# Cross stage of a perceiver layer: two score groups back to back, Strassen products in three PSUM banks

## The chip, the cores and the metric

The kernel is one launch on one core of a Trainium2 chip. The metric is the device time in microseconds. Lower is better. TensorE is called PE here, VectorE DVE, ScalarE ACT, GpSimd POOL and SyncE SP, as in the profile.

## The reference

The program is one layer with three parts, each added to a residual stream `x` of 256 rows by 512 features: cross attention over a context of 25088 rows, self attention with a learned bias, and a mixture of 8 experts. The change touches the first part alone:

```
q = layernorm(x) @ Wq.T + bq          # 256 x 512, 8 heads of 64
k = ctx @ Wk.T + bk                   # 25088 x 512
v = ctx @ Wv.T + bv                   # 25088 x 512
attn = softmax(q k^T / sqrt(64))      # per head, over the 25088 rows
x = x + attn @ v
```

The functions are float32. The kernel carries each factor of a product as two float16 parts, high and low, and makes a product from three float16 matmuls (high by high, low by high, high by low).

## The kernel before, in words

**Tiling.** The context comes in 49 chunks of 512 rows. For each chunk PE makes K (512 features by 512 rows) and V (512 by 512). Each is a 2 by 2 block product made in the Winograd form of Strassen's scheme: seven products M1, M5, M6, M2, M7, M3, M4 in that order (`unit`, L1600), each of 12 matmuls of 256 columns, and block sums between them. A product adds onto what its PSUM bank holds, so the sums need few extra instructions: `seed` (ACT, L761) copies M1's bank into a second one, `copy_m5` (ACT, L774) takes M5 into the SBUF tile `m5_f`, `add_u4` (DVE, L1194) and `add_c22` (DVE, L1207) add it to others. The four result blocks C11, C22, C12, C21 are then split: `block_highs` (ACT, L782) writes the float16 high part and `block_lows` (DVE, L1179) the low part.

**Attention per chunk.** The 8 heads go in four groups of two (g = 0 to 3). For a group, `scores` (PE, L1660) makes the logits of two heads in two PSUM banks, each head on one half of the array's rows (64 by 128). `maxima` (DVE, L1159) finds the row maxima and updates the running one, `exps` (ACT, L807) takes the exponentials with their row sums (4 instructions), `p_highs` (ACT, L820) and `p_lows` (DVE, L1173) split the probabilities, SP transposes both parts by DMA into `pt_s` (`turn_p`, L463), and `weigh` (PE, L1680) multiplies them with V two groups later, into `ps_o`. `add_o` (DVE, L1213) adds a pair of groups to the accumulator after POOL has rescaled it.

**Context.** The sums and the splits of the chunk two steps ahead are made by POOL (`ctx_parts`, L583: four sums and seven low parts per chunk) with high parts from ACT (`ctx_highs`, L708). In its order POOL then does `rescale` (L610) and `step_max` (L628), whose `dmax` ACT needs for `alphas` (L799).

**Order.** A step c works on the attention of chunk c and the products of chunk c + 1, and has two halves: in h = 0 (the K half) the products of K stand between groups 0 and 1, in h = 1 (the V half) those of V between groups 2 and 3. The order on each engine is written out by hand in its own `step`, and every engine runs its list in order. What joins them are semaphores; the waits that matter here are

```
elif m == M4:                                   # PE, unit, L1617
    pe.wait_ge(c22_done, g - 1)
...
dve.wait_ge(p_high, NG * c + g + 1)             # DVE, p_lows, L1175
...
if n in (3, 5):                                 # POOL, ctx_lows, L578
    pool.wait_ge(t_high, 2 * k - 1 + n // 5)
...
act.wait_ge(dmax_done, n + 1)                   # ACT, alphas, L802
```

M4 waits for `add_c22` of its own half, since it adds onto a bank that `add_c22` reads. PSUM has eight banks: `ps_proj` has four (the Strassen products), `ps_s` two (scores) and `ps_o` two (outputs). Steps 0 to 47 have both scores and products; step 48, the last, is written out apart (`last_step`).

Of the kernel before, what the change touches and what calls it, by code (L numbers as in the profile page):

```python
# [156 lines left out]
def layer(nc, x, ctxt, wq, wk, wv, bv, cols, w_in_dram, wg, w1, w2, w3, out):  # L157
    with ExitStack() as ctx:
# [42 lines left out]
        m5_f = sb("m5_f", [P, 2, QUARTER], F32, cross)  # L201
        q_s = [sb(f"q_s{k}", [P, NG, T], F16, cross) for k in range(2)]
# [149 lines left out]
        def score_bank(c, g, head):  # L352

            return ps_proj[:, head, :] if isinstance(c, int) and c == LAST and g % 2 else ps_s[:, head, :]

# [46 lines left out]
        C11, C22, C12, C21 = (0, 0, 0), (3, 1, 1), (2, 0, 1), (1, 1, 0)  # L402
# [297 lines left out]
        def _(act):  # L700
# [1279 lines left out]
```

## Time and profile before

| | |
|---|---|
| median of 3 runs | 1519.84 us (1518.81 to 1520.62) |
| the profiled execution, its own time | 1517.86 us |
| its span | 1516.1 us |
| PE busy | 1452.8 us, 96% of the span |
| VectorE busy | 1298.2 us, 86% |
| ScalarE busy | 1254.2 us, 83% |
| GpSimd busy | 951.0 us, 63% |
| mean granted PE clock | 0.984 of full speed |
| one step of the cross stage (605.38 to 629.98) | 24.60 us |
| in it PE, VectorE, ScalarE, GpSimd busy | 24.60, 21.50, 21.86, 18.84 us |

The cross stage is about the first 1240 us. The last row but one is the distance between the same scores instruction of two steps, and the last row is the busy time of each engine in that stretch: PE has no idle time there, and the others have three to six microseconds each.

### The profile page before, as it was taken

Reading aid. Unit: us, or ns where it says so; the run is one execution under the profiler, and the core shown is the slowest. Engines: PE = TensorE matmul, PEld = TensorE weight load, DVE = VectorE, ACT = ScalarE, POOL = GpSimd, SP = SyncE. Lnnn points to the kernel's source line nnn. Section 1 sums busy time; section 2 is a strip of 40 time slices with the busy share of each in tenths; the row PEclk is TensorE's granted clock in tenths of the full one; section 3 lists DMA queues with packets and bytes.
Section 4 is the critical chain, followed back from the end, with each engine's and each line's share of the span. In section 5 each row is a group of like instructions: output and inputs, shape, how many; then the busy total and the mean of one; then the engine's idle time right before and its main releaser. Section 6 shows DMA issues by size and latency. Waiting matters only on the chain.

```text
span 1516.1 us, 47982 instructions
## 1 busy us (share of the span) xinstructions
PE 1452.8 (96%) x17942; PEld 1206.2 (80%) x17942; DVE 1298.2 (86%) x1768; ACT 1254.2 (83%) x3039; POOL 951.0 (63%) x980
## 2 busy tenths in 40 slices
PE   6999999999999999999999999999999887599999
PEld 5788888888888888888888888888888764377776
DVE  6788989888888888898888888888889887788995
ACT  4788888888888888888888888888988875666883
POOL 6586877778687878787777878787878522500000
PEclk9999999999999999999999999999999998699999
DMA  4357555565656565655556565656566578766991
GB/s 187 71 110 143 115 135 133 122 138 117 143 113 139 111 143 112 139 119 134 135 116 143 113 145 111 138 111 145 112 137 130 116 154 223 175 232 241 337 329 46
DMA packets 460175, 220.40 MB, mean 145 GB/s; under 512 B 433856, under 2 KB 440000, under 8 KB 453328
## 3 DMA queue, kind: packets, MB, share of 16 engines
q1 hardware_dynamic: 459680, 218.22, 59.6%
q10 hardware_dynamic: 432, 1.32, 0.3%
q8 instruction: 43, 0.70, 0.2%
q14 instruction: 20, 0.16, 0.0%
HBM read 111.96 MB, written 0.56 MB: 74 GB/s over the span
## 4 chain that ended last, share of the span: by engine, by line
PE 85%; DVE 6%; DMA 3%; ACT 2%; POOL 2%; issue 1%; SPq 0%; DVEq 0%; ACTq 0%; POOLq 0%
PE ps_proj L1626 55%; PE ps_s L1676 9%; PE ps_o L1694 8%; PE ps_proj L1895 6%; PE ps_o L1911 3%; DMA pt_s<-p_s 2%; DVE wsp L1375 2%; PE ps_proj L1655 1%; POOL ctx_s L580 1%; DVE cmax L1163 1%; DVE p_s L1176 1%; PE ps_proj L1911 1%; DMA ctx_f<-ctxt_dram 1%; ACT prob L815 0%; PE ps_o L1596 0%
## 5 line engine op out<-in xcount | busy, mean ns | idle before, releaser
L1626 PE MATMUL ps_proj<-ctx_s,wk_s 128*128 128x256 f16 x4032 | 480.6, 273 | 3.9 <-ACT ps_proj L769 3.6
L1626 PE MATMUL ps_proj<-wv_s,ctx_s 128*128 128x256 f16 x4032 | 480.6, 273 | 1.5 <-ACT ps_proj L771 1.5
L580 POOL TENSOR_TENSOR ctx_s<-t_f,ctx_s 128x512 f16<-128x512 f32 x192 | 265.0, 1390 | 279.9 <-ACT ctx_s L717 279.9
L1626 PEld LDWEIGHTS ps_proj<-ctx_s,wk_s 128*128 128x128 f16 x4032 | 379.9, 98 | 66.4 <-issue 24.3
L1626 PEld LDWEIGHTS ps_proj<-wv_s,ctx_s 128*128 128x128 f16 x4032 | 379.9, 98 | 63.4 <-issue 11.4
L815 ACT ACTIVATE prob<-ps_s,nmax 128x256 f32<-128x256 f32 x776 | 357.1, 476 | 8.3 <-DVE nmax L1170 8.1
L1163 DVE TENSOR_REDUCE cmax<-ps_s 128x4 f32<-128x1024 f32 x194 | 237.5, 1224 | 123.9 <-PE ps_s L1676 123.9
L1176 DVE SCALAR_TENSOR_TENSOR p_s<-prob,p_s 128x1024 f16<-128x1024 f32 x196 | 320.3, 1634 | 0.7 <-ACT p_s L826 0.7
L580 POOL TENSOR_TENSOR ctx_s<-ctx_f,ctx_s 128x512 f16<-128x512 f32 x144 | 215.7, 1498 | 10.3 <-ACT ctx_s L712 5.4
L826 ACT ACTIVATE p_s<-prob 128x1024 f16<-128x1024 f32 x196 | 206.6, 1054 | 6.7
L1694 PE MATMUL ps_o<-v_s,pt_s 128*128 128x64 f16 x4704 | 171.6, 194 | 15.2 <-DMA pt_s<-p_s 15.2
L1694 PEld LDWEIGHTS ps_o<-v_s,pt_s 128*128 128x128 f16 x4704 | 165.2, 99 | 23.0 <-DMA pt_s<-p_s 17.8
L1676 PE MATMUL ps_s<-k_s,q_s 64*128 64x256 f16 x2328 | 160.7, 271 | 2.7 <-ACT prob L815 2.6
L815 ACT ACTIVATION_READ_ACCUMULATOR prob<-ps_s,nmax 128x1 f32 x776 | 161.6, 208 | 0.0
L1676 PEld LDWEIGHTS ps_s<-k_s,q_s 64*128 64x128 f16 x2328 | 97.5, 94 | 52.9 <-issue 39.1
L1185 DVE TENSOR_TENSOR v_s<-ps_proj,v_s 128x512 f16<-128x512 f32 x192 | 127.5, 686 | 11.4 <-ACT v_s L791 7.9
L1375 DVE SCALAR_TENSOR_TENSOR wsp<-wst,wsp 128x1024 f16<-128x1024 f32 x95 | 116.9, 1240 | 9.7 <-ACT wsp L947 9.4
L791 ACT ACTIVATE v_s<-ps_proj 128x512 f16<-128x512 f32 x192 | 108.9, 600 | 16.4 <-PE ps_proj L1626 16.4
L566 POOL TENSOR_TENSOR t_f<-ctx_f,t_f 128x512 f32<-128x512 f32 x48 | 104.8, 2184 | 0.0
L622 POOL TENSOR_TENSOR o_acc<-o_acc,alpha 128x512 f32<-128x512 f32 x98 | 103.0, 1051 | 0.0
L717 ACT ACTIVATE ctx_s<-t_f 128x1024 f16<-128x1024 f32 x96 | 100.6, 1048 | 0.1
L947 ACT ACTIVATE wsp<-wst 128x1024 f16<-128x1024 f32 x96 | 99.3, 1046 | 0.0
(235 smaller groups left out, 1800.4 us busy)
## 6 DMA issues: line engine op xcount, KB each, us to landing
ctx_f<-ctxt_dram SPq DMA_DIRECT2D x48, 1024.0 KB, 5.4
wst<-w_dram SPq DMA_DIRECT2D x96, 512.0 KB, 5.5
pt_s<-p_s SPq DMA_TRANSPOSE x408, 3.1
tisa<-tisa_scores SPq DMA_DIRECT2D x12, 256.0 KB, 5.7
w_in_f<-w_in_dram SPq DMA_DIRECT2D x2, 1024.0 KB, 6.2
w_f<-wk_dram SPq DMA_DIRECT2D x2, 512.0 KB, 6.4
ctx_f<-ctxt_dram SPq DMA_DIRECT2D x2, 512.0 KB, 7.8
w_f<-wv_dram SPq DMA_DIRECT2D x1, 1024.0 KB, 11.3
```

Source lines behind the costliest of these rows:

```text
L566: pool.tensor_tensor(out=t2, in0=b22, in1=t1, op=ALU.subtract).then_inc(t_sum, 1)
L580: pool.tensor_tensor(out=low[:, n, :, :], in0=sources[n], in1=high[:, n, :, :], op=ALU.subtract).then_inc(ctx_low, 1)
L791: ins = act.activation(out_v(0, odd, i, j), ps, ACT.Copy)
L815: ins = act.activation(prob[:, g % 2, (2 * b + r) * HC:(2 * b + r + 1) * HC], score_bank(c, g, b)[:, r * HC:(r + 1) * HC], ACT.Exp, bias=n ...
L826: act.activation(p_s[:, g % 2, 0, :], prob[:, g % 2, :], ACT.Copy, scale=P_SCALE).then_inc(p_high, 1)
L1163: dve.tensor_reduce(cmax[:, g % 2, :], ps.rearrange("p b (r k) -> p (b r) k", r=2), AX, ALU.max).then_inc(cmax_done, 1)
L1176: dve.scalar_tensor_tensor(out=p_s[:, g % 2, 1, :], in0=prob[:, g % 2, :], scalar=P_SCALE, in1=p_s[:, g % 2, 0, :], op0=ALU.mult, op1=ALU. ...
L1185: ins = dve.tensor_tensor(out_v(1, odd, i, j), ps, out_v(0, odd, i, j), ALU.subtract)
L1375: dve.scalar_tensor_tensor(out=weights(1, j)[:, n, :], in0=wst[:, j % 4, n, :], scalar=FW_SCALE, in1=weights(0, j)[:, n, :], op0=ALU.mult, ...
L1626: ins = pe.matmul(ps_proj[:, bank(h, role), sub * QUARTER:(sub + 1) * QUARTER], lhsT, rhs, start=(fresh and sub == 0 and t == 0 and i == 0 ...
L1676: ins = pe.matmul(score_bank(c, g, head)[:, r * HC:(r + 1) * HC], q_s[a][rows, g, r * P:(r + 1) * P], k_s[odd][b][rows, g, r * HC:(r + 1) ...
L1694: ins = pe.matmul(ps_o[:, vg // 2, col:col + DK], pt_s[:, vg, a, 4 * head + tile, :], v_s[vodd][b][:, tile, u * DK:(u + 1) * DK], start=(i ...
```

## The change

- **Scores.** Groups 2h and 2h + 1 are scored back to back, the even one in `ps_s`, the odd one in `ps_o` (`score_banks`). PE's half step becomes M1, scores, scores, M5, M6, weigh, M2, weigh, M7, M3, M4.
- **Outputs.** `weigh` writes one bank, `ps_proj[3]`, for both pairs (`out_bank`), and waits for the `add_o` of the pair before.
- **Strassen.** The products use three banks. M5 goes to the bank of role 2 and waits for the C21 low part of the half before; C22 is summed into the SBUF tile `c22_f`.
- **ScalarE.** Per half: C21, alphas, seed, context high, copy of M5, both groups' exps, C11, p_highs of the even group, the high part of the context sums (`sum_highs`, split off `ctx_highs`), p_highs of the odd group, C22, C12. p_highs of the odd group stood in the next half before.
- **VectorE.** Per half: C21, add_o, both maxima, add_u4, p_lows of the even group, add_c22, C11, p_lows of the odd group, C22, C12.
- The last step follows the same banks; the bias scores and the dummy matmuls of `keep_busy` move to other banks.

```diff
+        c22_f = sb("c22_f", [P, 2, QUARTER], F32, cross)
...
-        def score_bank(c, g, head):
...
+        def score_banks(c, g):
+
+            if isinstance(c, int) and c == LAST and g >= 2:
+                return (ps_proj[:, 0:2, :], ps_s[:, :, :])[g - 2]
+            return (ps_s[:, :, :], ps_o[:, :, :])[g % 2]
+
+        def out_bank(c, half):
+
+            return ps_o[:, 0, :] if isinstance(c, int) and c == LAST and half else ps_proj[:, 3, :]
...
-        M1, M5, M6, M2, M7, M3, M4 = (0, 0, 0), (3, 3, 3), (4, 4, 1), (1, 1, 0), (5, 5, 1), (6, 2, 2), (2, 6, 1)
+        M1, M5, M6, M2, M7, M3, M4 = (0, 0, 0), (3, 3, 2), (4, 4, 1), (1, 1, 0), (5, 5, 1), (6, 2, 2), (2, 6, 1)
...
-                g, ps = 2 * k + h, half_bank(bank(h, role))
+                g, ps = 2 * k + h, c22_f[:, :, :] if which == C22 else half_bank(bank(h, role))
...
-                    if strassen:
-                        seed(c + 1, h)
-                    pc, pg = back(c, 2 * h, 1)
-                    if exists(pc, 0):
-                        p_highs(pc, pg)
                     if exists(c, -1) and h == 0:
                         alphas(c - 1, 1)
                     if exists(c, 0) and h == 1:
                         alphas(c, 0)
                     if strassen:
+                        seed(c + 1, h)
+                    if exists(c, 2):
+                        ctx_highs(c + 2, odd, h)
+                    if strassen:
                         copy_m5(c + 1, h)
                     if exists(c, 0):
                         exps(c, 2 * h, odd)
+                        exps(c, 2 * h + 1, odd)
+                    if strassen:
+                        block_highs(c + 1, h, C11, 1 - odd)
                     if exists(c, 0):
                         p_highs(c, 2 * h)
-                    if strassen:
-                        block_highs(c + 1, h, C11, 1 - odd)
                     if exists(c, 2):
-                        ctx_highs(c + 2, odd, h)
+                        sum_highs(c + 2, odd, h)
                     if exists(c, 0):
-                        exps(c, 2 * h + 1, odd)
+                        p_highs(c, 2 * h + 1)
...
-                dve.tensor_tensor(half_bank(bank(h, 3)), half_bank(bank(h, 1)), m5_f[:, :, :], ALU.add).then_inc(c22_done, 1)
+                dve.tensor_tensor(c22_f[:, :, :], half_bank(bank(h, 1)), m5_f[:, :, :], ALU.add).then_inc(c22_done, 1)
...
-                    if exists(c, 0):
-                        maxima(c, 2 * h, odd)
-                    pc, pg = back(c, 2 * h, 1)
-                    if exists(pc, 0):
-                        p_lows(pc, pg)
-                    if strassen:
-                        add_u4(c + 1, h)
                     if exists(c, -1):
                         add_o(c - 1, h)
                     if exists(c, 0):
+                        maxima(c, 2 * h, odd)
                         maxima(c, 2 * h + 1, odd)
+                    if strassen:
+                        add_u4(c + 1, h)
+                    if exists(c, 0):
+                        p_lows(c, 2 * h)
                     if strassen:
                         add_c22(c + 1, h)
                         block_lows(c + 1, h, C11, 1 - odd)
                     if exists(c, 0):
-                        p_lows(c, 2 * h)
+                        p_lows(c, 2 * h + 1)
...
                 elif m == M5:
-                    pe.wait_ge(block_low, 4 * g - 2 + (2 if isinstance(k, int) and g == 2 else 0))
+                    pe.wait_ge(block_low, 4 * g)
...
-                elif g >= 1 or after(c, -1):
+                elif g % 2 == 0 and (g or after(c, -1)):
                     pe.wait_ge(exp_done, NG * c + g)
...
-                if vg % 2 == 0 and after(vc, -1):
-                    pe.wait_ge(added, 2 * vc + vg // 2 - 1)
+                if isinstance(vc, int) and vc == LAST and vg == 2:
+                    pe.wait_ge(exp_done, NG * LAST + 2)
+                elif vg % 2 == 0 and (vg or after(vc, -1)):
+                    pe.wait_ge(added, 2 * vc + vg // 2)
...
+                    units(M1)
+                    if exists(c, 0):
+                        scores(c, 2 * h, odd)
+                        scores(c, 2 * h + 1, odd)
+                    units(M5, M6)
+                    weighted(0)
+                    units(M2)
+                    weighted(1)
+                    units(M7, M3, M4)
```

**VectorE, the K half inside the loop.** L1163 and L1169 are the maxima, L1170 and L1176 (of the change) the running maximum, L1211 and L1217 `add_c22`, L1188 and L1194 the C11 lows, L1176 (before) and L1182 `p_lows`. Buffer numbers are left out of the names here and in the profile: `m_f` is `m5_f`, `c_f` is `c22_f`. Before:

```order
L1161 REGISTER_ALU
L1163 TENSOR_REDUCE cmax<-ps_s 128x4 [waits s_done]
L1170 SCALAR_TENSOR_TENSOR nmax<-cmax,nmax 128x2x2 [waits cmax_done]
L1210 REGISTER_ALU
L1211 TENSOR_TENSOR ps_proj<-ps_proj,m_f 128x512 [waits unit_done]
L1183 ISA
L1188 SCALAR_TENSOR_TENSOR k_s<-ps_proj,bk_s,k_s 128x256 [waits block_high]
L1188 SCALAR_TENSOR_TENSOR k_s<-ps_proj,bk_s,k_s 128x256
L1176 SCALAR_TENSOR_TENSOR p_s<-prob,p_s 128x1024 [waits p_high]
L1183 REGISTER_ALU
L1191 TENSOR_TENSOR k_s<-ps_proj,k_s 128x2x256 [waits block_high]
L1183 REGISTER_ALU
```

The change:

```order
L1176 SCALAR_TENSOR_TENSOR nmax<-cmax,nmax 128x2x2 [waits cmax_done]
L1203 ISA
L1204 REGISTER_ALU [waits unit_done]
L1207 SCALAR_TENSOR_TENSOR ps_proj<-ps_proj,bk_d,m_f 128x256 [waits m5_done]
L1207 SCALAR_TENSOR_TENSOR ps_proj<-ps_proj,bk_d,m_f 128x256
L1182 SCALAR_TENSOR_TENSOR p_s<-prob,p_s 128x1024 [waits p_high]
L1216 REGISTER_ALU
L1217 TENSOR_TENSOR c_f<-ps_proj,m_f 128x512 [waits unit_done]
L1189 ISA
L1194 SCALAR_TENSOR_TENSOR k_s<-ps_proj,bk_s,k_s 128x256 [waits block_high]
L1194 SCALAR_TENSOR_TENSOR k_s<-ps_proj,bk_s,k_s 128x256
L1182 SCALAR_TENSOR_TENSOR p_s<-prob,p_s 128x1024 [waits p_high]
```

`add_c22` stood right behind the maxima of the odd group. It now stands behind `p_lows` of the even group, which waits for `p_high`.

**ScalarE, the K half inside the loop.** L815 and L822 are the exps, L826 and L833 `p_highs`, L794 and L801 the C11 highs, L712 the context highs, L717 and L724 the highs of the context sums. Before:

```order
L815 ACTIVATE prob,lsum<-ps_s,nmax 128x256 [waits scaled]
L815 ACTIVATE prob,lsum<-ps_s,nmax 128x256 x3
L826 ACTIVATE p_s<-prob 128x1024 [waits turned_p2,exp_done]
L789 REGISTER_ALU
L794 ACTIVATE k_s<-ps_proj,bk_s 128x256 [waits unit_done]
L794 ACTIVATE k_s<-ps_proj,bk_s 128x256
L711 ISA
L712 ACTIVATE ctx_s<-ctx_f 128x1024 [waits ctx_loaded0]
L716 ISA
L717 ACTIVATE ctx_s<-t_f 128x1024 [waits t_sum]
L809 REGISTER_ALU
L815 ACTIVATE prob,lsum<-ps_s,nmax 128x256 [waits nmax_done]
```

The change:

```order
L822 ACTIVATE prob,lsum<-ps_s,nmax 128x256 x3
L816 REGISTER_ALU
L822 ACTIVATE prob,lsum<-ps_o,nmax 128x256 [waits nmax_done]
L822 ACTIVATE prob,lsum<-ps_o,nmax 128x256 x3
L796 REGISTER_ALU
L801 ACTIVATE k_s<-ps_proj,bk_s 128x256 [waits unit_done]
L801 ACTIVATE k_s<-ps_proj,bk_s 128x256
L832 ISA [waits exp_done]
L833 ACTIVATE p_s<-prob 128x1024 [waits turned_p2]
L723 ISA
L724 ACTIVATE ctx_s<-t_f 128x1024 [waits t_sum]
L833 ACTIVATE p_s<-prob 128x1024 [waits turned_p3,exp_done]
```

The even group's `p_highs` stood right behind its own four exps; eight exps and the C11 highs now stand ahead of it. The highs of the context sums stand behind it.

**PE, the end of the K half, of the change.** L1700 is `weigh`, L1629 the products M2, M7, M3 and M4 (the last row):

```order
L1629 MATMUL ps_proj<-ctx_s,wk_s 128x256 [waits ctx_low]
L1629 MATMUL ps_proj<-ctx_s,wk_s 128x256 x11
L1700 MATMUL ps_proj<-v_s,pt_s 128x64 [waits turned_p3]
L1700 MATMUL ps_proj<-v_s,pt_s 128x64 x23
L1611 REGISTER_ALU
L1629 MATMUL ps_proj<-ctx_s,wk_s 128x256 [waits u4_done,ctx_low]
L1629 MATMUL ps_proj<-ctx_s,wk_s 128x256 x11
L1611 REGISTER_ALU
L1629 MATMUL ps_proj<-ctx_s,wk_s 128x256 [waits ctx_low]
L1629 MATMUL ps_proj<-ctx_s,wk_s 128x256 x11
L1611 REGISTER_ALU
L1629 MATMUL ps_proj<-ctx_s,wk_s 128x256 [waits c22_done,ctx_low]
```

The products M7, M3 and M4 are now consecutive; M4 waits for `c22_done`, as before.

## Rows read from the trace of the kernel before

**Rows 1.** Stretch; busy of PE, PEld, DVE, ACT, POOL; PEclk, DMA share, GB/s.

```profile
605.38:629.98 24.60, 24.60 (x313) 20.93 (x312) 21.50 (x29) 21.86 (x56) 18.84 (x20) 1.00 0.58 128
```

**Rows 2.** Chain of waits, half a step; columns: start, us, what, instructions.

```profile
647.86 0.76 PE ps_s L1676 x12
648.62 2.73 PE ps_proj L1626 x24
651.34 0.70 PE ps_o L1694 x24
652.04 2.62 PE ps_proj L1626 x24
```

**Rows 3.** Timeline, PE, last step: two score groups back to back, then another.

```profile
1238.05 0.83 PE L1676 MATMUL ps_s<-k_s,q_s 64*128 64x256 f16 x12
...
1238.71 0.82 PE L1676 MATMUL ps_proj<-k_s,q_s 64*128 64x256 f16 x12
...
1239.46 1.89 PE L1587 MATMUL ps_proj<-tisa_e,tsel 128*16 128x512 f32 x4
```

**Rows 4.** Timeline, K half, PE and ScalarE; columns: start, us, engine, line.

```profile
642.48 0.81 ACT L769 ACTIVATE ps_proj<-ps_proj,bk_s 128x256 f32<-128x256 f32 x2 [0.80 <-DVE v_s L1185]
...
643.05 2.79 PE L1626 MATMUL ps_proj<-ctx_s,wk_s 128*128 128x256 f16 x24
...
644.15 0.21 ACT L805 ACTIVATE alpha<-dmax 128x8 f32<-128x8 f32 x1
...
644.65 0.60 ACT L780 ACTIVATE m_f<-ps_proj 128x512 f32<-128x512 f32 x1 [0.29 <-PE ps_proj L1626]
```

**Rows 5.** Timeline, ScalarE, later in the same half.

```profile
648.11 0.82 ACT L794 ACTIVATE k_s<-ps_proj,bk_s 128x256 f16<-128x256 f32 x2
...
648.82 1.05 ACT L712 ACTIVATE ctx_s<-ctx_f 128x1024 f16<-128x1024 f32 x1
...
649.77 1.05 ACT L717 ACTIVATE ctx_s<-t_f 128x1024 f16<-128x1024 f32 x1
...
650.71 0.47 ACT L815 ACTIVATE prob<-ps_s,nmax 128x256 f32<-128x256 f32 x1
...
652.51 1.59 ACT L796 ACTIVATE k_s<-ps_proj 128x512 f16<-128x512 f32 x3
```

**Rows 6.** Timeline, same half: VectorE beside GpSimd.

```profile
643.76 1.27 POOL L563 TENSOR_TENSOR t_f<-ctx_f 128x512 f32<-128x512 f32 x1
...
644.51 0.54 DVE L1170 SCALAR_TENSOR_TENSOR nmax<-cmax,nmax 128x4 f32<-128x4 f32 x1
...
649.92 0.16 DVE L1170 SCALAR_TENSOR_TENSOR nmax<-cmax,nmax 128x4 f32<-128x4 f32 x1
...
650.07 0.70 DVE L1211 TENSOR_TENSOR ps_proj<-ps_proj,m_f 128x512 f32<-128x512 f32 x1
...
651.08 3.25 POOL L580 TENSOR_TENSOR ctx_s<-t_f,ctx_s 128x512 f16<-128x512 f32 x2
...
651.46 1.85 DVE L1176 SCALAR_TENSOR_TENSOR p_s<-prob,p_s 128x1024 f16<-128x1024 f32 x1
```

**Rows 7.** VectorE's p_lows, 500 to 1000 us: duration ns min/median/max.

```profile
L1176 DVE SCALAR_TENSOR_TENSOR p_s<-prob,p_s x81: 1209/1840/2374, 503.8 to 996.0; 128x1024 f16<-128x1024 f32 x81
```

**Rows 8.** Timeline, GpSimd: end of the K half, and the V half.

```profile
655.60 0.20 POOL L635 TENSOR_TENSOR dmax<-nmax 128x8 f32<-128x8 f32 x1
...
662.50 1.16 POOL L580 TENSOR_TENSOR ctx_s<-t_f,ctx_s 128x512 f16<-128x512 f32 x1 [5.58 <-ACT ctx_s L717]
...
663.61 2.19 POOL L580 TENSOR_TENSOR ctx_s<-ctx_f,ctx_s 128x512 f16<-128x512 f32 x1
...
668.20 0.20 POOL L635 TENSOR_TENSOR dmax<-nmax 128x8 f32<-128x8 f32 x1
```

**Rows 9.** Two stretches outside the steady part; PE busy, PEclk, DMA share, GB/s.

```profile
1190.00:1202.00 12.00, 10.41 (x135) 1.00 0.41 78
1298.00:1310.00 12.00, 4.44 (x136) 0.50 0.80 132
```

More of the change, by code:

```diff
@@ L399, in out_v @@
             return v_s[odd][kk][:, 2 * j:2 * j + 2, i * QUARTER:(i + 1) * QUARTER]
-        C11, C22, C12, C21 = (0, 0, 0), (3, 1, 1), (2, 0, 1), (1, 1, 0)
+        C11, C22, C12, C21 = (0, 0, 0), (None, 1, 1), (2, 0, 1), (1, 1, 0)
         def half_bank(n):
@@ L715, in ctx_highs, with sum_highs @@
                     act.activation(ctx_s[odd][0][:, 2, :, :], ctx_f[odd][:, 2:4, QUARTER:CH], ACT.Copy).then_inc(ctx_high, 1)
+            def sum_highs(k, odd, half):
                 act.wait_ge(t_sum, 4 * k - 1 + half)
@@ L1181, in block_lows @@
                 role, i, j = which
-                g, ps = 2 * k + h, half_bank(bank(h, role))
+                g, ps = 2 * k + h, c22_f[:, :, :] if which == C22 else half_bank(bank(h, role))
                 dve.wait_ge(block_high, 4 * g + 1 + (C11, C22, C12, C21).index(which))
@@ L1218, in add_o @@
                 acc = o_acc[:, half, :, :, :].rearrange("p u r d -> p (u r d)")
-                dve.tensor_tensor(acc, acc, ps_o[:, half, :], ALU.add).then_inc(added, 1)
+                dve.tensor_tensor(acc, acc, out_bank(c, half), ALU.add).then_inc(added, 1)
             def by_rows(t, half):
@@ L1295, in last_step @@
                 block_lows(LAST, 1, C21, LAST % 2)
+                add_o(LAST - 1, 0)
                 maxima(LAST, 0, LAST % 2)
-                p_lows(LAST - 1, 3)
                 maxima(LAST, 1, LAST % 2)
-                add_o(LAST - 1, 0)
                 tisa_scores()
                 p_lows(LAST, 0)
+                maxima(LAST, 2, LAST % 2)
                 add_o(LAST - 1, 1)
-                maxima(LAST, 2, LAST % 2)
                 p_lows(LAST, 1)
@@ L1712, in units, with weighted @@
                                 unit(c + 1, 1 - odd, h, m)
-                    for half, before, between, behind in ((0, (M1,), (M5, M6), (M2,)), (1, (), (M7, M3), (M4,))):
-                        g = 2 * h + half
-                        units(*before)
-                        if exists(c, 0):
-                            scores(c, g, odd)
-                        units(*between)
-                        vc, vg = back(c, g, PV_LAG)
-                        if exists(vc, 0):
-                            weigh(vc, vg, odd if g >= PV_LAG else 1 - odd)
-                        units(*behind)
+                    def weighted(half):
+                        vc, vg = back(c, 2 * h + half, PV_LAG)
+                        if exists(vc, 0):
+                            weigh(vc, vg, odd if 2 * h + half >= PV_LAG else 1 - odd)
+                    units(M1)
[7 more added lines that the diff above has]
+                    units(M7, M3, M4)
             def last_step():
@@ L1729, in last_step @@
                 scores(LAST, 1, odd)
+                scores(LAST, 2, odd)
                 tisa_scores()
                 weigh(LAST - 1, 2, 1 - odd)
-                scores(LAST, 2, odd)
                 weigh(LAST - 1, 3, 1 - odd)
@@ L1742, in keep_busy @@
                 for _ in range(count):
[L1743 removed]
+                    pe.matmul(ps_proj[:, 0, :], w_in_s[K][0][:, 0, 0:P], w_in_s[K][0][:, 1, :], start=True, stop=True)
             pe.wait_ge(w_in_low[K], 2)
```

32 lines of the change are left out of this document (15 added, 17 removed).

## The prediction

> **What bounds the kernel now.** I read the stretches first. In one step of the cross stage's steady part PE is busy in all of its 24.60 us, at the full granted clock, while VectorE is busy for 21.50, ScalarE for 21.86 and GpSimd for 18.84 [rows 1]. So a step lasts as long as its PE instructions. The question for the change is therefore double: how much PE time it removes, and whether PE still finds everything ready. The chain of waits gives PE's pieces [rows 2]: one score group 0.76 us, 24 product matmuls 2.73 us when a score group stands ahead of them and 2.62 us otherwise (1.31 a product), a weigh 0.70. The timeline gives the durations on the other engines and, more important, what starts when.
>
> **What PE saves.** A score group uses the array in halves of 64 rows and every other matmul here all 128, and the rows show a price at each change of form. In the last step two score groups already stand back to back: the first takes 0.66 us, the second 0.75 [rows 3]. So joining two groups saves 0.10 in the scores and 0.11 in the products behind them [rows 2], 0.21 per half, 0.4 per step. With nothing else, a step would take 24.2 us.
>
> **What the new order asks of the other engines.** The two order listings show the point. M4 must wait for `add_c22`. Before, VectorE did it right behind the odd group's maxima. Now `p_lows` of the even group is ahead of it, and that needs `p_highs` of the even group, which ScalarE reaches only after the copy of M5, eight exps and C11. All of this begins with the scores of the same half, and the next half's scores come behind M4. It is a closed loop, and PE is in it only for short pieces. Around it, starting at the end of `p_highs`:
> - `p_lows` 1.21 if GpSimd is out of its way [rows 7], and at that moment it is: it waits for `sum_highs`, the instruction behind `p_highs`;
> - `add_c22` 0.70 [rows 6];
> - M4 and M1, 1.31 each [rows 2], two score groups 1.41 [rows 3];
> - from M5's start to the start of its copy 1.60 [rows 4], the copy 0.50 to the next start (0.60, less the 0.10 by which ScalarE's instructions overlap, as 648.82 and 649.77 show [rows 5]);
> - eight exps 3.60, since four take 1.80 from first start to what follows [rows 5];
> - C11 0.72 in the K half, and 0.50 in the V half (one instruction, as the three at 652.51 take 1.59) [rows 5];
> - `p_highs` 1.05, of the same form as the context sums at 649.77 [rows 5].
>
> That is 13.2 us in a V half and 13.4 in a K half, or 26.6 a step, though PE has only 24.2 us of work. Seen from PE, M4 could start about 9.4 us after the scores (1.41 + 2.62 + 0.70 + 1.31 + 0.70 + 2.62) and `add_c22` ends at 1.41 + 1.60 + 0.50 + 3.60 + 0.72 + 1.05 + 1.21 + 0.70 = 10.8. **M4 waits 1.4 us in each half.** Next, M5 now waits for the C21 low of the half before. VectorE reaches it through `add_c22`, C11, `p_lows` of the odd group, C22, C12 and C21: five instructions of 0.6 to 0.7 like `add_c22` [rows 6] and one of 1.2 to 2.3 [rows 7], 4.5 to 5.6 us against PE's 4.7 (0.70 + 1.31 + 1.31 + 1.41). I add 0 to 0.7 a half for it and for handovers between engines, which the pieces above leave out, and take 13.5 for the half from K to V.
>
> **The second loop runs through GpSimd.** `sum_highs` moves behind eight exps and `p_highs`. In its order GpSimd can do `rescale` and `dmax` only after the low parts that wait for `sum_highs`, and the alphas, now ahead of the seed, of the context highs and of the copy of M5 on ScalarE, wait for `dmax`. In the V half GpSimd sat idle 5.58 us for the highs of the sums and then took from 662.50 to 668.40, 5.90 us, up to the end of `dmax` [rows 8]. From the V half to the K half the loop is 5.90, alphas 0.2 [rows 4], seed 0.71 (0.81 less the overlap) [rows 4], context highs 0.95 [rows 5], copy 0.50, exps 3.60, C11 0.72, `p_highs` 0.95, `sum_highs` 1.05: 14.6 us, more than the first loop's 13.2. From K to V it is 651.08 to 655.80, 4.72 [rows 6, 8], then 0.2, 0.5, 0.5, 0.5, 3.60, 0.50, 0.95, 1.05 (the seed and the context highs are half as large or one instruction there): 12.5, so there the first loop decides.
>
> VectorE and GpSimd also get into each other's way. The running maximum started at 644.51 and ended at 645.05, when GpSimd's sum from 643.76 ended (645.03); the next one, with GpSimd idle at its start, took 0.16 [rows 6]. `p_lows` took 1.21 at best and 1.84 in the middle [rows 7], and GpSimd's two low parts beside one took 3.25 [rows 6] where one alone takes 1.16 [rows 8]. The 5.90 already contains one such wait (2.19 instead of 1.16 [rows 8]). In the new K half the four context sums begin right after `dmax`, exactly when both running maxima come, on which the exps wait. Each may lose from nothing to one sum, 1.27 [rows 6]; together they delay the exps by 0 to 1.2. I take 0.7, and 15.3 us from V to K.
>
> The Trainium skill, page "SBUF — State Buffer", section "Who interferes with whom", says that a VectorE instruction with two SBUF inputs and a GpSimd instruction that reads SBUF take turns on a shared port, and that the later one waits for the whole of the other. The trace agrees, with the 0.54 and the 0.16. By that rule the added term may be all of 1.2; if the two only shared bandwidth, it would be nearly nothing.
>
> **Edits with no price of their own.** C22 in SBUF costs VectorE's sum the same 0.70 at most, and its low part gains a second SBUF input, which can cost up to one GpSimd instruction (in the range above). One output bank: `add_o` (about 0.7) stands at the start of VectorE's half, and weigh comes 4.0 us after the scores, so it is covered. The transposes of the even group have a whole half, those of the odd group some 6 us. ScalarE loses the idle 0.1 us between exps and `p_highs`; it isn't the bound. The last step has PE waiting on ScalarE already; one `p_lows` less and one group of exps earlier there are worth -2 to +2, taken as 0.
>
> **Sum.** 15.3 + 13.5 = 28.8 us a step against 24.60: +4.2, in the 46 steps that also prepare context (with step 0 counted apart, and step 47, which has no context work). 46 x 4.2 = 193, plus 2 x 2.4 for those two, by the first loop with handovers (27.0): +198 us. The profiled execution took 1517.86 (span 1516.1); it would take 1716. The median of the runs shown is 2 us above it, so **1718 us**. From both sides: with the first loop alone, and no handovers, 26.6 a step, 48 x 2.0 = +96, 1616; with every collision in both halves 15.8 + 14.1 = 29.9, 46 x 5.3 + 5 = +249, 1769.
>
> **Rivals.**
> - *Only the M4 loop counts.* GpSimd starts its lows early enough and nothing collides: 26.6 to 27.0 a step, 1616 to 1635. For it: GpSimd is busy only 18.84 of 24.60 us [rows 1]. Against it: that idle time was one wait for `sum_highs` [rows 8], and this instruction moves back. 14%.
> - *The change gives what PE saves.* M4 finds C22 ready and the step falls to 24.2: 48 x 0.4 = -19, 1501. This is the faster side. It decides if `add_c22` ends within 9.4 us of the scores, 1.4 less than my sum; the eight exps alone are 3.6 of it, with no slack to find. 4%.
> - *Something in between*, most of M4's wait absorbed: 1515 to 1610. 5%.
> - *PE's clock falls.* PE would be busy 24.2 of 28.8 us, 84%. At 87% the granted clock stayed 1.00, at 37% it was 0.50 [rows 9], that is 1.2 GHz instead of 2.4. The Trainium skill, "TensorE: Matmul & The Clock Gate", section "Part 1: The HAM clock gate", says that an idle PE is put back to the half clock. In rows: at a mean of 0.8 the 5.3 us of PE pieces in each half's loop grow by 1.3, 2.6 a step, +125, about 1840. The waits are short and spread, so 5%.
> - The forecast: 72%.
>
> **Numbers.** A difference of 0.2%, 3 us, is about what a measurement of this kernel can tell from none. Slower: 72 + 14 + 5 and most of the in-between, 94%; same 2%; faster 4%. The range goes from the first loop alone to all collisions, 1616 to 1769, rounded to 1620 and 1770; it leaves out the clock, the in-between and the faster case, 14%.
>
> **What would show it.** PE busy about 84% in the steady part, with PE idle ahead of one product per half, released by VectorE's `add_c22` (over 1 us each); VectorE idle some 3 us ahead of the even `p_lows`, released by ScalarE's `p_highs`; ScalarE idle ahead of the alphas, released by GpSimd's `dmax`; score groups back to back in 1.41 us; V to K scores further apart than K to V. I am wrong on the first loop if VectorE doesn't wait for `p_high`, on the second if alphas never wait, and wrong altogether if PE stays at 100% busy.

## The result and the profile after

The changed kernel takes **1762.78 us** (median of 4 runs, 1762.46 to 1772.35) against 1519.32 for the kernel before in the same session: ratio 1.1618, 95% interval 1.1578 to 1.1659. It is slower, as forecast. The forecast was 1718; the time lies inside the range of 1620 to 1770, near its upper end. The profiled execution took 1762.66 us, +244.8 on the one of before.

Stretches of the changed kernel, columns as in [rows 1]: a K half and a V half of one step, then those of a later step.

```profile
612.84:628.35 15.51, 12.30 (x157) 10.56 (x157) 11.96 (x16) 11.48 (x29) 12.55 (x14) 1.00 0.43 72
628.35:641.80 13.45, 12.39 (x157) 10.46 (x156) 10.08 (x14) 10.57 (x27) 6.32 (x7) 1.00 0.65 153
701.23:718.41 17.18, 13.97 (x157) 11.34 (x157) 13.60 (x19) 11.50 (x29) 14.21 (x17) 0.90 0.42 88
718.41:731.66 13.25, 12.26 (x157) 10.54 (x156) 8.50 (x11) 10.58 (x27) 4.65 (x4) 1.00 0.61 120
```

So there are two kinds of step: 28.96 us, and, in 19 of the 48, about 30.4. PE does the same work in both (157 matmuls a half). In the first kind it is busy for 12.3 us of 15.5 and for 12.4 of 13.4, 85% of the step, where 84% was forecast.

The waits of the changed kernel from 100 to 1400 us; columns: who waits, for whom, us in total, times, longest.

```profile
POOL ctx_s L584 <- ACT ctx_s L724: 467.8, 88, 8.6
DVE p_s L1182 <- ACT p_s L833: 296.9, 88, 3.7
ACT alpha L812 <- POOL dmax L639: 233.1, 87, 3.4
...
PE ps_proj L1629 <- DVE c_f L1217: 123.9, 86, 2.0
PE ps_proj L1629 <- DVE v_s L1191: 53.7, 43, 1.3
```

All three waits of the forecast are there in nearly every one of the about 90 halves: VectorE's `p_lows` for ScalarE, ScalarE's alphas for GpSimd, and M4 (PE for `c_f`) for VectorE. The last row is a fourth wait, of M5 for the C21 low part of the half before, in the K halves. The timeline shows how they hang together, in the K half that begins at 701.23 and the V half behind it.

```profile
701.23 0.83 PE L1680 MATMUL ps_s<-k_s,q_s 64*128 64x256 f16 x12
...
701.89 0.82 PE L1680 MATMUL ps_o<-k_s,q_s 64*128 64x256 f16 x12
...
703.96 2.78 PE L1629 MATMUL ps_proj<-ctx_s,wk_s 128*128 128x256 f16 x24 [1.25 <-DVE v_s L1191]
...
704.03 0.21 ACT L812 ACTIVATE alpha<-dmax 128x8 f32<-128x8 f32 x1 [3.41 <-POOL dmax L639]
...
705.91 0.60 ACT L787 ACTIVATE m_f<-ps_proj 128x512 f32<-128x512 f32 x1
...
706.60 0.47 ACT L822 ACTIVATE prob<-ps_s,nmax 128x256 f32<-128x256 f32 x1
...
711.87 1.10 ACT L724 ACTIVATE ctx_s<-t_f 128x1024 f16<-128x1024 f32 x1
...
712.06 1.22 DVE L1182 SCALAR_TENSOR_TENSOR p_s<-prob,p_s 128x1024 f16<-128x1024 f32 x1 [3.29 <-ACT p_s L833]
...
713.05 2.36 POOL L584 TENSOR_TENSOR ctx_s<-t_f,ctx_s 128x512 f16<-128x512 f32 x2 [2.89 <-ACT ctx_s L724]
...
714.03 2.43 PE L1629 MATMUL ps_proj<-ctx_s,wk_s 128*128 128x256 f16 x12 [1.96 <-DVE c_f L1217]
...
716.25 2.22 PE L1629 MATMUL ps_proj<-wv_s,ctx_s 128*128 128x256 f16 x12
...
718.41 0.83 PE L1680 MATMUL ps_s<-k_s,q_s 64*128 64x256 f16 x12
...
719.83 2.79 PE L1629 MATMUL ps_proj<-wv_s,ctx_s 128*128 128x256 f16 x24
...
726.86 1.11 ACT L724 ACTIVATE ctx_s<-t_f 128x1024 f16<-128x1024 f32 x1
...
728.94 1.48 PE L1629 MATMUL ps_proj<-wv_s,ctx_s 128*128 128x256 f16 x12 [0.99 <-DVE c_f L1217]
```

The two score groups take 1.42 us where M5 follows without a wait (718.41 to 719.83), 1.41 in [rows 3]. The alphas come 2.80 us behind the scores, the copy of M5 (705.91) 1.67 later than the 3.01 behind the scores that PE alone would allow, and M4 is late by 1.96. M4 and M1 then take 2.22 and 2.16 us from start to start: PE's granted clock, 0.90 over this half, is down here (0.61 from 714.03 to 718.41, 1.00 from 705 to 714). In the other kind of step the same two take 1.31 and 1.40:

```profile
625.64 1.47 PE L1629 MATMUL ps_proj<-ctx_s,wk_s 128*128 128x256 f16 x12 [1.96 <-DVE c_f L1217]
...
626.95 1.47 PE L1629 MATMUL ps_proj<-wv_s,ctx_s 128*128 128x256 f16 x12
```

### The profile page after: what moved, and what is told of

Its sections match the earlier page's. It is cut to its first block, busy times and chain, and to the rows that moved or that the text cites. A ratio compares the mean times of both kernels' runs of the same rounds, so it can differ in the third digit from the quotient of the medians.

```text
span 1760.9 us, 47836 instructions
## 1 busy us (share of the span) xinstructions
PE 1492.4 (85%) x17942; PEld 1234.1 (70%) x17942; DVE 1323.8 (75%) x1768; ACT 1262.3 (72%) x3039; POOL 953.9 (54%) x980
## 4 chain that ended last, share of the span: by engine, by line
issue 45%; POOL 34%; PE 12%; DVE 4%; ACT 2%; DMA 1%; POOLq 1%; SPq 1%; DVEq 0%; ACTq 0%
POOL ctx_s L584 19%; PE ps_proj L1905 5%; POOL l_acc L624 5%; POOL t_f L570 3%; POOL t_f L567 3%; PE ps_o L1921 2%; DVE wsp L1378 1%; PE ps_proj L1658 1%; POOL l_acc L629 1%; DMA pt_s<-p_s 1%; POOL dmax L639 1%; ACT prob L822 1%; PE ps_proj L1921 1%; DMA ctx_f<-ctxt_dram 1%; POOL t_f L572 0%
## 5 line engine op out<-in xcount | busy, mean ns | idle before, releaser
L1629 PE MATMUL ps_proj<-ctx_s,wk_s 128*128 128x256 f16 x4032 | 495.3, 278 | 156.2 <-DVE c_f L1217 93.9
L1182 DVE SCALAR_TENSOR_TENSOR p_s<-prob,p_s 128x1024 f16<-128x1024 f32 x196 | 313.8, 1601 | 328.9 <-ACT p_s L833 328.9
L1629 PEld LDWEIGHTS ps_proj<-ctx_s,wk_s 128*128 128x128 f16 x4032 | 387.4, 99 | 228.3 <-issue 180.6
L1629 PE MATMUL ps_proj<-wv_s,ctx_s 128*128 128x256 f16 x4032 | 502.4, 280 | 48.2 <-DVE c_f L1217 39.3
L1629 PEld LDWEIGHTS ps_proj<-wv_s,ctx_s 128*128 128x128 f16 x4032 | 392.2, 101 | 125.8 <-DVE c_f L1217 51.5
L833 ACT ACTIVATE p_s<-prob 128x1024 f16<-128x1024 f32 x196 | 216.2, 1105 | 0.3 <-DMA pt_s<-p_s 0.3
L822 ACT ACTIVATE prob<-ps_s,nmax 128x256 f32<-128x256 f32 x392 | 180.0, 475 | 9.6 <-DVE nmax L1176 4.8
L1700 PE MATMUL ps_proj<-v_s,pt_s 128*128 128x64 f16 x4656 | 168.9, 194 | 17.3 <-DMA pt_s<-p_s 17.1
L1700 PEld LDWEIGHTS ps_proj<-v_s,pt_s 128*128 128x128 f16 x4656 | 161.7, 98 | 27.1 <-DMA pt_s<-p_s 21.7
L822 ACT ACTIVATE prob<-ps_o,nmax 128x256 f32<-128x256 f32 x388 | 179.9, 499 | 0.0
L584 POOL TENSOR_TENSOR ctx_s<-ctx_f,ctx_s 128x512 f16<-128x512 f32 x144 | 167.1, 1160 | 3.9 <-ACT ctx_s L716 3.9
L1169 DVE TENSOR_REDUCE cmax<-ps_s 128x4 f32<-128x1024 f32 x98 | 119.2, 1216 | 8.1 <-PE ps_s L1680 8.1
L1169 DVE TENSOR_REDUCE cmax<-ps_o 128x4 f32<-128x1024 f32 x97 | 118.1, 1217 | 0.0
L724 ACT ACTIVATE ctx_s<-t_f 128x1024 f16<-128x1024 f32 x96 | 106.0, 1104 | 0.0
L624 POOL TENSOR_TENSOR l_acc<-l_acc,alpha 128x8 f32<-128x8 f32 x98 | 87.4, 892 | 28.1 <-ACT alpha L812 28.1
L1191 DVE TENSOR_TENSOR v_s<-ps_proj,v_s 128x512 f16<-128x512 f32 x144 | 94.0, 677 | 0.0
```

Of the source, the lines that this page charges most:

```text
L584: pool.tensor_tensor(out=low[:, n, :, :], in0=sources[n], in1=high[:, n, :, :], op=ALU.subtract).then_inc(ctx_low, 1)
L624: pool.tensor_tensor(out=l_acc[:, cols], in0=l_acc[:, cols], in1=alpha[:, cols], op=ALU.mult).then_inc(l_step, 1)
L724: act.activation(ctx_s[odd][0][:, 3 + 2 * half:5 + 2 * half, :, :], t_f[:, 2 * half:2 * half + 2, :, :], ACT.Copy).then_inc(t_high, 1)
L833: act.activation(p_s[:, g % 2, 0, :], prob[:, g % 2, :], ACT.Copy, scale=P_SCALE).then_inc(p_high, 1)
L1169: dve.tensor_reduce(cmax[:, g % 2, :], score_banks(c, g).rearrange("p b (r k) -> p (b r) k", r=2), AX, ALU.max).then_inc(cmax_done, 1)
L1182: dve.scalar_tensor_tensor(out=p_s[:, g % 2, 1, :], in0=prob[:, g % 2, :], scalar=P_SCALE, in1=p_s[:, g % 2, 0, :], op0=ALU.mult, op1=ALU. ...
```

## Experiments

Every one is an edit of the changed kernel. Times of e1 to e8 and e10 to e12 are of one run; the kernel before took 1517.7 beside e1 to e4, 1519.1 beside e5 to e8, and 1517.3 (median of 17) beside e9 to e12. The four runs of the change lie 10 us apart, so a difference of a few us between single runs says nothing.

PE's clock has a part in most of these differences. Its mean over the span was 0.962 in the change, 0.938 in e1, 0.981 in e2, 0.937 in e3, 0.979 in e4, 0.958 in e5, 0.961 in e6, 0.980 in e7, 0.983 in e10, 0.982 in e11 and 0.962 in e12.

**e1: `add_c22` ahead of the even low part.**

```diff
-                    if exists(c, 0):
-                        p_lows(c, 2 * h)
                     if strassen:
                         add_c22(c + 1, h)
                         block_lows(c + 1, h, C11, 1 - odd)
+                    if exists(c, 0):
+                        p_lows(c, 2 * h)
```

> The change, but VectorE does add_c22 and the C11 low part ahead of p_lows of the even group. In the changed kernel M4 waited 1.96 us (K half) and 0.99 us (V half) for add_c22. Theory of two loops (the prediction's): M4's wait goes, but from V to K the loop through GpSimd (sum_highs, low parts, rescale, dmax, alphas) still sets the pace, and the later p_lows of the even group collide with GpSimd; a step stays between 28 and 29.4 us, the time between 1700 and 1760. Rival (M4's wait is the whole cost): the step falls by both waits, about 3 us, to 26 or less, the time below 1640.

Measured: **1814.5 us**, slower than the change by 52. Every theory missed upward. M4's wait is gone; M5's took its place (PE and VectorE from 600 to 634 us):

```profile
604.13 2.78 PE L1629 MATMUL ps_proj<-ctx_s,wk_s 128*128 128x256 f16 x24 [2.49 <-DVE v_s L1191]
...
618.49 4.27 PE L1629 MATMUL ps_proj<-wv_s,ctx_s 128*128 128x256 f16 x24 [2.21 <-DVE k_s L1197]
...
628.20 3.68 DVE L1182 SCALAR_TENSOR_TENSOR p_s<-prob,p_s 128x1024 f16<-128x1024 f32 x2
...
631.81 1.64 DVE L1191 TENSOR_TENSOR v_s<-c_f,v_s 128x512 f16<-128x512 f32 x1
```

The C22, C12 and C21 lows stand behind both `p_lows`, which now come late and together, beside GpSimd. M5 waits for C21, since with three banks it goes where C21 was. So VectorE's queue can close a third loop. It isn't alone here: the alphas still wait for `dmax`, up to 5.0 us.

Most of the 52 us seems to be the clock, though. In the V half shown M5 and M6 take 4.27 us, where 2.78 is usual (604.13). Its step is 14.63 and 16.03 us, and all steady steps of e1 last 30.6 to 30.7. Without the 1.5 us of the clock that would be about 29.2, an estimate from these rows, against 28.96 in the change.

**e2: GpSimd does `rescale` and `dmax` ahead of the lows that wait for the sums.** Only lows 0 and 1 stay ahead; the other five follow `step_max`.

> The change, but GpSimd does rescale and dmax ahead of the low parts that wait for sum_highs. Theory of two loops: ScalarE's wait for dmax ahead of the alphas (3.41 us in the K half, 1.34 in the V half) goes, but the M4 loop through VectorE's p_lows stays at 13.2 to 13.5 a half and the clock episodes with it; 26.6 to 29 us a step, 1625 to 1740. Rival (M4's wait is the whole cost and GpSimd only follows): nothing changes, 1763 within 5.

Measured: **1766.2 us**, no gain, although the alphas wait for `dmax` no more. From 300 to 1100 us (the line numbers are 6 higher here) the next instruction, the seed, waits instead, for VectorE's C12 low:

```profile
ACT ps_proj L782 <- DVE v_s L1197: 68.6, 27, 2.5
ACT ps_proj L784 <- DVE k_s L1203: 66.5, 27, 2.5
```

The halves are 15.26 and 14.41 us, 29.67 a step against 28.96. The wait for GpSimd had hidden one for VectorE of nearly the same length. The time is the same all the same, because the clock no longer falls: it is 1.00 from 200 to 1100 us, although M4 still waits up to 1.7 us and M5 up to 1.3.

**e3: both edits.**

> Both edits. Theory of two loops: each alone gives little and both together clearly more than the sum of their gains, 25 to 27.7 us a step, 1540 to 1670; what is left is ScalarE's and VectorE's own order and their collisions with GpSimd. Rival (one cause): the same as the better of the two edits alone.

Measured: **1816.5 us**. The seed waits up to 4.1 us, M5 up to 3.0, both for VectorE's lows; the mean clock is 0.937. M4 and the alphas wait no more. Halves in which the clock doesn't fall last 14.6 (K) and 14.4 us (V), 29.0 together. With two loops opened, the third alone is as slow as all, in this order of VectorE, which also puts the even low part back; e11 has the third loop by itself.

**e4: dummy matmuls in M4's wait.** They keep PE busy until `add_c22` is nearly done (M4 still waits up to 0.5 us); their results are not used.

```diff
-                    units(M7, M3, M4)
+                    units(M7, M3)
+                    if exists(c, 0) and exists(c, 1):
+                        pe.wait_ge(exp_done, NG * c + 2 * h + 2)
+                        for _ in range(14 if h == 0 else 7):
+                            pe.matmul(ps_s[:, 0, 0:QUARTER], wk_s[0][:, 0, 0, 0:P], wk_s[0][:, 1, 0, :], start=True, stop=True)
+                    units(M4)
```

> The change, with 14 dummy matmuls of 256 columns ahead of M4 in a K half and 7 in a V half, into a score bank that has been read, so that PE isn't idle while M4 waits. Their results are used by nobody. In the changed kernel K halves last 15.52 or, in runs of several steps, 17.18 us, and in the long ones M4 and the next M1 take 2.2 us instead of 1.3 and 1.4. Theory: the long ones are PE's clock falling to half after M4's wait; with the wait filled all K halves last about 15.5, a step 28.97, the time about 1730. Rival: the two lengths come from collisions of VectorE and GpSimd, or the dummies cost as much as they save; then 1755 to 1790.

Measured: **1737.4 us**, 25.3 less than the profiled execution of the change. In the steady part the halves are 15.54 and 13.46, 29.0 a step; the 30.4 us steps are gone. From 600 to 800 us the change had the clock at 0.97, e4 has 1.00:

```profile
600.00:800.00 200.00, 185.43 (x2305) 159.15 (x2304) 151.35 (x193) 151.72 (x390) 130.21 (x132) 1.00 0.51 109
```

This is the price of the clock by itself: the loops are as long as before, only PE's idle time is filled.

**e5: VectorE's odd low part behind C22 and C12** (ScalarE's order unchanged).

> The change, but VectorE does p_lows of the odd group behind the C22 and C12 low parts instead of ahead of them. The first two kernels left one thing in common: M5 of the next half waits for the C21 low part, which is behind both p_lows of its half. Theory of two loops (M4 and GpSimd; M5's wait a small term): little, 1735 to 1765. New theory (the binding loop is VectorE's queue as a whole: exps, p_highs, both p_lows, C22, C12, C21, M5, its copy, exps): C21 is not freed by this, since it still stands behind the odd p_lows at the start of the next half; so also little, 1730 to 1800. This run tells the place of C22 and C12 from that of C21.

Measured: **1777.7 us**. M5 waits 0.7 us at most now, the halves are 15.52 with 13.86 or 17.17 with 13.26. The alphas still wait up to 3.4 us and M4 up to 2.1: the other two loops are whole.

**e6: ScalarE rounds the even group between the two groups' exps.**

> The change, but ScalarE does p_highs of the even group between the two groups' exps, as the kernel before did; everything else as changed (scores back to back, three banks). p_lows of the even group, and behind it add_c22, can start 2.5 us earlier (1.80 + 0.72). M4 loop theory: M4's waits go entirely and a step loses the 3 us of them, to 26 or 27 us, about 1640. GpSimd or VectorE theory: sum_highs and the odd p_lows stay where they are, so the step stays at 28 to 29.5 and only the clock episodes may go: 1700 to 1745.

Measured: **1740.9 us**, 22 less. M4 no longer waits; M5 waits up to 2.2 for the C21 low and the alphas up to 4.0 for `dmax`.

**e7: the odd group put off.** Its exps come behind the even rounding, its rounding and low part in the next half as before the change, and the sum rounding stands ahead of the copy of M5. Besides, `add_c22` and C11 stand ahead of the even low part on VectorE, and the odd group's maxima behind `add_u4`.

> Same scores, banks and PE order as the change; ScalarE and VectorE reordered: p_highs and p_lows of the odd group go to the next half, right behind C21; sum_highs goes ahead of the copy of M5; exps of the odd group go behind p_highs of the even one; C11 and add_c22 go ahead of p_lows of the even group. Theory of VectorE's queue and GpSimd together: both loops are cut, PE is again busy nearly all the time, a step 24.2 to 25.5 us, the time 1500 to 1565. Rival (three banks and M5's wait for C21 are what costs): a step stays above 27, 1640 or more.

Measured: **1614.3 us**: halves of about 12.5 (K) and 13.8 us (V), clock 1.00 from 300 to 1100 us. The alphas wait no more. PE waits for the transposes of the odd group, which now come too late (up to 2.1 us for `pt_s`, 46.2 us in all from 300 to 1100 us).

**e8: three moves together.** The sum rounding goes first in the half, right behind the C21 high part; the even rounding goes between the groups' exps; the odd rounding and the odd low part go last in the half, behind C12. The context highs and the seed go ahead of the alphas with the sum rounding.

```
ScalarE: C21, sum_highs, ctx_highs, seed, alphas, copy of M5, exps even, p_highs even,
         exps odd, C11, C22, C12, p_highs odd
VectorE: C21, add_o, maxima, maxima, add_u4, p_lows even, add_c22, C11, C22, C12, p_lows odd
```

> Same scores, banks and PE order; sum_highs right behind C21 on ScalarE, exps of the odd group behind p_highs of the even one, p_highs and p_lows of the odd group last in their own half, add_c22 still behind the even p_lows. GpSimd theory: with sum_highs at the start its loop is cut, 24.5 to 26.5 us a step, 1515 to 1610. M5 theory (odd p_lows ahead of C21 keeps M5 waiting): above 27 a step, 1640 or more.

Measured: **1525.1 us** against 1519.1 before. The steady halves are 12.09 (V) and 12.22 or 12.42 (K), 24.42 us a step against the 24.60 of before. It lost the gain outside: in step 0 ScalarE waited 7.1 us for GpSimd's first sums, and in a late step 3.0 and 3.3 us for the bias table's preparation behind the odd low part.

**e9: e8 with those two places mended.**

```diff
+                    first = isinstance(c, int) and c == 0 and h == 0
+                    if exists(c, 2) and not first:
                         sum_highs(c + 2, odd, h)
...
+                    if exists(c, 2) and first:
+                        sum_highs(c + 2, odd, h)
                     if strassen:
                         block_highs(c + 1, h, C22, 1 - odd)
...
+                    if isinstance(c, int) and c == LOOP_END + 1:
+                        tisa_args(h)
                     if exists(c, 0):
                         p_lows(c, 2 * h)
```

In step 0 the sum rounding stands where it stood. In the late step VectorE prepares the bias table (`tisa_args`) ahead of the even low part, and ScalarE's exponential of it stands ahead of C11.

> The order of e8 (sum rounding first in a half, even split between the two exponentials, odd split last), with two places outside the steady stretch mended: in the first half of step 0 the sum rounding stands where it stood, since there ScalarE waited 7.1 us for GpSimd's sum (first half 22.5 us against 13.6 before), and the time-interval exponential of the one late step no longer stands behind the odd split (ScalarE waited 3.0 us there, PE 2.7). The steady halves of e8 were 12.09 and 12.22 to 12.43, 24.4 us a step against 24.60 before. If the steady gain of 0.18 us x 42 steps = 8 us was only covered by those two places (some 9 and 2 to 3 us), this gives 1511 to 1517, faster than before by 0.2 to 0.5%. Rival: the longer distance from the odd split to its transposes costs at both ends of the loop whatever is mended, 1519 to 1525.

Measured, in 12 runs beside 17 of the kernel before (1517.29): **1511.55 us** (1510.16 to 1515.04), ratio **0.9962, interval 0.995 to 0.9974**. It is faster than the kernel before, by 0.4%. Two steps of it:

```profile
605.21:654.21 49.00, 48.49 (x627) 42.52 (x626) 44.38 (x57) 43.45 (x113) 34.46 (x38) 1.00 0.59 127
```

24.50 us a step, of which PE works 24.24: the 24.2 that the prediction worked out as PE's part alone, against 24.60 [rows 1]. In 200 to 1100 us the one wait of PE that remains is

```profile
PE ps_proj L1637 <- DVE v_s L1196: 8.2, 19, 0.4
```

The next three each take one of the three moves back.

**e10: sum rounding late again.** The seed and the context highs go behind the alphas again too, as in the change; so this is two things at once, both on the second loop.

> e9 with one of its three moves taken back: the sum rounding stands behind both exponentials and the even split again. If the loop over GpSimd (sum rounding, GpSimd's lows, difference of maxima, alphas, seed, context rounding, exponentials) bounds by itself, alphas waits for the difference of maxima for 2 to 4 us in each half, the step is 26.5 to 28 and the time 1600 to 1690. If VectorE's queue (the odd split ahead of the C12 and C21 lows) was what really bound, no such wait stays and the time is within 10 us of e9.

Measured: **1724.1 us**, more than the 1690 expected; halves 15.13 and 13.9 to 14.1. In 200 to 1100 us:

```profile
ACT alpha L812 <- POOL dmax L639: 212.9, 62, 4.0
```

ScalarE waits for nothing else in this stretch, and the clock is 1.00. So from one sum rounding over GpSimd and the alphas to the next the loop is closed, 29.1 us a step.

**e11: odd group's rounding and low part ahead of C22 and C12 again.**

> e9 with another move taken back: the odd split of a half stands ahead of the C22 and C12 splits again on both engines, as in the change. If VectorE's queue bounds by itself, the seed waits for the C12 low, or the M5 product for the C21 low, 0.5 to 2 us a half, the step is 25.5 to 28 and the time 1560 to 1680. If the other two moves were what mattered, within 10 us of e9.

Measured: **1581.9 us**, halves of 12.83 to 13.29, 26.0 to 26.1 us a step; M5 waits up to 0.6 us for C21, M4 up to 0.8 for `c_f`.

**e12: even rounding behind both groups' exps again.**

> e9 with the third move taken back: ScalarE rounds the even group only behind the exponentials of both, as in the change. If the loop of the M4 product (even rounding, even low, C22 sum, M4, the rest of PE's half up to the scores, M5, its copy, eight exponentials, C11, rounding: 13.2 us by the sum of the prediction) bounds by itself, both halves are about 13.2, the step 26.4 and the time 1595 to 1615, with M4 waiting about 1 us for VectorE's sum in each half. If it had only been carried along by the other two, within 10 us of e9.

Measured: **1722.9 us**, 108 above the upper bound expected. The halves are 14.32 and 13.77, and 15.6 to 16.0 where the clock falls. One V half:

```profile
613.44 0.83 PE L1688 MATMUL ps_s<-k_s,q_s 64*128 64x256 f16 x12
...
616.38 0.60 ACT L787 ACTIVATE m_f<-ps_proj 128x512 f32<-128x512 f32 x1 [2.06 <-PE ps_proj L1637]
...
616.87 0.47 ACT L822 ACTIVATE prob<-ps_s,nmax 128x256 f32<-128x256 f32 x1
...
620.47 0.65 ACT L798 ACTIVATE v_s<-ps_proj 128x512 f16<-128x512 f32 x1
...
620.95 1.11 ACT L833 ACTIVATE p_s<-prob 128x1024 f16<-128x1024 f32 x1
...
622.10 2.21 DVE L1187 SCALAR_TENSOR_TENSOR p_s<-prob,p_s 128x1024 f16<-128x1024 f32 x1 [3.71 <-ACT p_s L833]
...
624.23 0.68 DVE L1222 TENSOR_TENSOR c_f<-ps_proj,m_f 128x512 f32<-128x512 f32 x1
...
624.97 1.48 PE L1637 MATMUL ps_proj<-wv_s,ctx_s 128*128 128x256 f16 x12 [1.98 <-DVE c_f L1222]
...
626.28 1.47 PE L1637 MATMUL ps_proj<-ctx_s,wk_s 128*128 128x256 f16 x12
...
627.69 0.83 PE L1688 MATMUL ps_s<-k_s,q_s 64*128 64x256 f16 x12
```

This is the first loop of the prediction, alone and closed: 2.94 + 0.49 + 3.60 + 0.48 + 1.15 + 2.13 + 0.74 + 1.31 + 1.41 = 14.25 us. The sum was 13.2; the one term that differs is `p_lows`, 2.21 instead of 1.21, since with the earlier sum rounding GpSimd is at work beside it (a sum of 1.27 us starts at 621.96). In the change GpSimd was waiting then. This V half is one of the longer ones, behind a fall of the clock. The usual ones of 13.77 us have a shorter collision:

```profile
652.30 1.64 DVE L1187 SCALAR_TENSOR_TENSOR p_s<-prob,p_s 128x1024 f16<-128x1024 f32 x1 [3.70 <-ACT p_s L833]
```

In the K half `p_lows` takes 1.22, and instead the exps wait 0.6 us for a running maximum of 1.0 to 1.1 us beside GpSimd's low parts. 28.1 us a step and the falls of the clock together make the miss.

## Why the prediction was right, point by point

- **PE's saving** was 0.4 us a step in the forecast. It is real: PE's busy time is 24.24 us a step in e9, and a half in which PE waits for nothing lasts 12.09 us there against 12.30 before, the 0.21 of the forecast.
- **First loop, M4 behind the even rounding.** The V half from 718.41 lasts 13.25 us; the sum was 13.2. M4's wait was put at 1.4 in each half and is 0.99 there, 1.96 in the K half. e12 shows that this loop bounds by itself.
- **Second loop, sum rounding, GpSimd, alphas.** From one sum rounding to the next it takes 14.99 us from K to V (711.87 to 726.86), and the rest of that 30.4 us step, 15.4, from V to K, where 15.3 was forecast. In the steps without a clock fall K to V is 13.52, with 13.5 forecast:

```profile
623.47 1.11 ACT L724 ACTIVATE ctx_s<-t_f 128x1024 f16<-128x1024 f32 x1
...
636.99 1.11 ACT L724 ACTIVATE ctx_s<-t_f 128x1024 f16<-128x1024 f32 x1
```

  e10 shows that it too bounds alone. In the prediction's signs I had its scores the wrong way round: the wait comes behind the K scores, so K to V scores are the far ones (15.5), not V to K.
- **Within it** the exps start 0.2 us after the copy of M5 allows, not the 0.7 of the collision term, while GpSimd's part grew, from the 5.90 read in [rows 8] to 6.40 (728.04 to 734.44, its low parts in the V half up to the end of `dmax`). In it `rescale`'s first instruction, 128 by 8 elements, takes a median of 0.92 us in the changed kernel and 0.20 before (300 to 1100 us):

```profile
L624 POOL TENSOR_TENSOR l_acc<-l_acc,alpha x54: 646/916/1191, 301.1 to 1090.3; 128x8 f32<-128x8 f32 x54
```

```profile
L620 POOL TENSOR_TENSOR l_acc<-l_acc,alpha x65: 198/202/206, 309.8 to 1097.2; 128x8 f32<-128x8 f32 x65
```

  The first line is of the changed kernel, the second of the kernel before. Behind the V half's sums it now meets VectorE's C22 low part, which reads `c22_f` in SBUF, and behind the K half's the odd low part:

```profile
700.98 1.64 DVE L1191 TENSOR_TENSOR v_s<-c_f,v_s 128x512 f16<-128x512 f32 x1
...
702.03 0.65 POOL L624 TENSOR_TENSOR l_acc<-l_acc,alpha 128x8 f32<-128x8 f32 x1
...
714.58 1.91 DVE L1182 SCALAR_TENSOR_TENSOR p_s<-prob,p_s 128x1024 f16<-128x1024 f32 x1
...
715.37 1.18 POOL L624 TENSOR_TENSOR l_acc<-l_acc,alpha 128x8 f32<-128x8 f32 x1
```

  Both times it ends just behind VectorE's instruction (702.68 and 702.62, 716.55 and 716.49). The two deviations, -0.5 and +0.5, nearly cancel, which is luck. By the Trainium skill, "SBUF — State Buffer", section "Who interferes with whom", one of the two engines waits for the other's whole instruction; these rows agree, and show that it can be GpSimd that waits.
- **Step and sum.** From the scores of step 0 to those of the last step it is 1433.3 us, against 1191.0 before: +242.3. A step is 28.96 measured, 28.8 forecast: 46 x 4.36 = 201 us for 193. The 19 slower steps cost about 27 more, by the clock: this is the term that was mis-sized. It had been a rival of 5% with 125 us, all or nothing. The waits of M4 are the same 1.96 us with and without the fall, and e4 gives 25.3 us for it. The remaining 14 stand where 4.8 was forecast. They lie at the two ends: step 0 takes 5.8 us more than before (M4 waits 4.4 there), and the last three steps ahead of the last 18.7 more together (M5 waits 4.1 and 5.2 for C21 low parts that stand behind the bias table's preparation on VectorE); the 46 x 4.36 holds 8.7 of these 24.5, and small differences in other steps take off the rest. Ahead of step 0 and behind the last scores it is another 2.5 instead of 0. Together 201 + 27 + 14 + 2.5 = 245. The range held although it left the clock out: its upper end was a step of 29.9 us with every collision, and the 28.96 measured left room for the clock's 27 us. That is luck.
- **A third loop was missed.** The prediction gave M5's wait for the C21 low 0 to 0.7 us and did not name the seed's wait for the C12 low. In the change M5 waits 1.25, hidden under the alphas. From the start of `add_c22` to the end of the C21 low part VectorE takes 6.1 us (728.19 to 734.25), not 4.5 to 5.6, since the C22 low part takes 1.64 instead of 0.7. The prediction named this collision and left it out of M5's term. Where the other loops are opened, these waits are 2.5 to 4.1 (e1 to e3). The rival "only the M4 loop counts", 1616 to 1635, could therefore not have come true by repairing GpSimd's order: e2 did this and stayed at 1766.
- **The rival "the change gives what PE saves"** needs a different order on ScalarE and VectorE. With it, e9 gives 5.7 of the 19 us against the kernel before: its steps take 24.50 instead of 24.2.

Left open: why the clock falls in runs of steps and not in others with the same waits, and not at all in e2 and e10 from 200 to 1100 us, where PE waits too.

## What to carry to other kernels

When work moves within an in-order engine's list, write down every closed chain that runs through the moved instruction, and its length, not only PE's waits: here each of three chains alone was longer than PE's 24.2 us a step (29.1, 26.0 and 28.1 in e10 to e12), and edits that opened one or two of them gained 22 us at best and lost up to 54 (e1 to e3, e5, e6), part of it by the clock. Put first in an engine's list what another engine waits for longest (the sum rounding), and last what has slack (the odd group), and then look at the first and last passes of the loop, where that order can be the wrong one (9 us in e8).

## What the runs showed of the hardware

- PE's granted clock fell in a kernel in which PE was busy for 85% of the span. It fell behind waits of 1.25 and 1.96 us in one half, in 19 of 48 steps, and the two products behind the second wait then took 4.38 us instead of 2.71. In other steps with the same waits it did not fall, and in e2, with waits of up to 1.7 and 1.3 us, in none from 200 to 1100 us. Filling M4's waits with unused matmuls removed the falls and 25 us (e4).
- The C22 low part of the V half, which now reads SBUF twice, took 1.64 us each of 27 times between 300 and 1100 us, with GpSimd at work beside it (700.98, GpSimd's low part from 699.93 to 702.06), and 0.68 in the K half.
- Two score groups joined save 0.21 us each time (12.30 us a half before, 12.09 in the V halves of e8 and e9); the rows of the last step had given the same.
